# Layer attention: new places among the steps for a sequence's small operations, the first sequence's row maxima in six PSUM banks, and its chunk projected sooner

## The chip, the cores and the metric

The kernel runs on one core of one Trainium2 chip. The metric is the device time of one execution in microseconds (us), the median of several. Engines are named as in the profile: PE is TensorE's matmuls, PEld its weight loads, DVE VectorE, ACT ScalarE, POOL GpSimd, SP the engine that issues the DMAs.

## The reference, cut to what matters

Sixteen sequences of 256 tokens with 128 features go through four layers of (mamba, norm, attention, norm, feed-forward), then a mixture of experts, a sparse attention and the experts again. The change touches the attention of the four layers and the order of two operations in every layer norm:

```python
for l in range(4):
    m = _mamba(x, ...)                                   # before the attention
    x = _ln(x + m, g1[l], be1[l])
    qkv = jnp.einsum('bsd,od->bso', x, W_qkv) + b_qkv     # 16 heads of 8 features
    scores = jnp.einsum('bhqd,bhkd->bhqk', q, k) * SCALE
    wts = jax.nn.softmax(scores, axis=-1)
    o = jnp.einsum('bhqk,bhkd->bhqd', wts, v)
    x = _ln(x + o @ W_ao.T + b_ao, g2[l], be2[l])
    x = x + gelu(x @ W_f1.T + b_f1) @ W_f2.T + b_f2
```

## The kernel before, in words

**What a sequence needs.** For each sequence `b` the attention does the following. `project_qk` multiplies queries and keys into PSUM bank 7, `evac_qk` adds the biases on the way out, POOL's `parts` splits the values into high and low parts, SP's `spill` writes them to a scratch in HBM and `scatter` reads them back as 24-row groups into one of four buffers `hqk[r]`. `row` multiplies queries by keys with the queries on the partitions, so that DVE can take the maximum over the keys for each of 16 heads (`two_maxima` over two banks at once, 1024 columns; `maxima` over one, 512 columns; `copied_maxima` over one that ACT's `copy_row` has moved to SBUF). POOL's `split_max` splits the maxima, PE's `maxima` transposes them into bank 7, ACT's `max_rows` copies them, SP's `send_max` sends them by two DMAs into two further rows of `hqk[r]`. `score` then multiplies keys by queries and these rows, so that the maximum is subtracted, ACT's `exps` takes the exponentials (1024 columns at a time, eight per sequence), and PE's `values` multiplies them by the values (four groups of 16 matmuls into bank 6), which `project_v` and `lay_v` made by way of bank 7. ACT's `raw` copies the sums, PE's `sums` spreads the denominators in bank 7, ACT's `reciprocal` takes a logarithm and an exponential of its negative, POOL's `divide` multiplies, PE's `out` projects into bank 7, DVE's `add_out` adds to `xa`.

**Steps and places.** `heads` runs one step per sequence, 0 to 15: step 0 apart, twelve in a loop of three times four, 13 to 15 apart. A step has eight places, p = 0 to 7. At each, PE issues four `row` matmuls of two heads of a sequence one or two ahead (banks 0 and 1) and four `score` matmuls of two heads of the sequence itself (banks 2 and 3, or 4 and 5), and then one small operation. At even p one `two_maxima` frees banks 0 and 1; at odd p `maxima` frees bank 0 and `copy_row` bank 1. So `row` at p waits for the maxima of p-1. All engines run their instructions in the order of the program, and every hand-over is a semaphore wait, so an operation's place is its place in each engine's queue. Bank 7 has one user at a time: q and k, v, denominators, transposed maxima and output take turns.

**The places before.** PE: `project_v(b+1)` at 0, `values(b-1, 3)` at 1, `project_qk(b+3)` at 2, `values(b, 0)` at 3, `sums(b-1)` at 4, `values(b, 1)` and `maxima(b+1)` at 5, `values(b, 2)` at 6, `out(b-1)` at 7. DVE: `lay_v` at 0, `evac_qk` at 3 (two instructions of 256 columns), `add_out` at 7. ACT: `raw` at 1, both halves of `reciprocal` at 4, `max_rows` after the exponentials of 5. POOL: `copy_x`, `split_max`, `parts`, `divide`. SP: `spill(b+3)`, `send_max(b+1)`, `scatter(b+3)`.

**Ahead of the steps.** q and k of sequences 0 to 2 and v of 0 are projected in hooks inside the norm before the attention (PE hooks at quad and chunk (0,2), (1,0), (1,2), (1,3), ACT's at (0,3), (1,1), (1,3)). In the norm, DVE multiplies each chunk (line 1740, or its `dst` form) and then scales and shifts it (line 1745); it takes the multiplication of the next chunk ahead of that. Then come all 16 heads' rows of sequence 0 and the first 8 of sequence 1, in banks 0 and 1 only, and `maxima(0)` among sequence 1's.

## Time and profile before

| | |
|---|---|
| times of the kernel before | 2674.94, 2678.55, 2682.89 us (median 2678.55) |
| the profiled execution's own time | 2679.11 us |
| its span | 2677.4 us, mean granted TensorE clock 0.908 of full |
| PE, PEld busy | 80%, 52% of the span |
| DVE, ACT, POOL busy | 62%, 60%, 26% |
| DMA, mean over the span | 64 GB/s |

The span is the whole program, with stages that have different limits. The four layers' head attention begins (first `row`) at 150, 598, 1046 and 1493 us and takes about 265 us each time. A timeline row reads: start, duration, engine, line, operation, output<-inputs, shape, count, and in brackets how long the engine had been idle and what ended that.

### The profile page before, as it was taken

How to read it: one execution, taken by the hardware profiler on the slowest of the kernel's cores; microseconds unless marked ns; L12 is line 12 of the kernel's file. 1: busy time of each engine (PE TensorE's matmuls, PEld its weight loads, DVE VectorE, ACT ScalarE, POOL GpSimd, SP SyncE). 2: the span in 40 equal slices, each digit the busy share in tenths (PEclk: the TensorE clock that was granted, in tenths of full speed). 3: DMA queues.
4: the chain of work that ended last, by engine and by line, in shares of the span. 5: the costliest groups of instructions: out<-in, count | busy, mean ns of one | idle time of the engine just before them, and what ended most of it. 6: DMA issues, size and time to landing. Idle time of an engine off the chain costs nothing.

```text
span 2677.4 us, 49462 instructions
## 1 busy us (share of the span) xinstructions
PE 2136.1 (80%) x15147; PEld 1401.1 (52%) x15147; DVE 1664.4 (62%) x2491; ACT 1618.9 (60%) x2604; POOL 700.9 (26%) x980
## 2 busy tenths in 40 slices
PE   6968889987888896888899688887877478886795
PEld 4534445643444663444475344454666347775584
DVE  4557775656775765777475577756643267767541
ACT  6447778745777763777784477886544214454461
POOL 0113221022231102223101233211757130004664
PEclk8969999996999997899999699998988789997897
DMA  3033320013331002333000333204141201004223
GB/s 114 10 96 107 110 74 7 9 45 92 110 100 50 16 0 81 94 100 108 20 9 10 96 97 112 81 7 88 46 118 53 70 0 32 1 9 93 79 90 128
DMA packets 116930, 171.73 MB, mean 64 GB/s; under 512 B 13728, under 2 KB 75168, under 8 KB 116512
## 3 DMA queue, kind: packets, MB, share of 16 engines
q1 hardware_dynamic: 107552, 150.66, 19.9%
q0 software_dynamic: 9216, 19.02, 2.0%
q8 instruction: 88, 1.44, 0.2%
q14 instruction: 74, 0.61, 0.1%
HBM read 85.19 MB, written 82.35 MB: 63 GB/s over the span
## 4 chain that ended last, share of the span: by engine, by line
PE 49%; DVE 14%; POOL 11%; issue 10%; DMA 6%; ACT 6%; SPq 1%; DVEq 1%; ACTq 0%; POOLq 0%
PE ps L829 8%; DVE hmx L1883 6%; POOL back_scratch L2420 6%; PE ps L861 5%; POOL slot_scratch L2415 5%; DMA hqk<-hmt 3%; PE ps L877 2%; ACT hrow L1489 2%; PE ps L762 2%; PE ps L726 2%; PE ps L732 2%; PE ps L677 2%; PE ps L683 2%; PE ps L1257 1%; PE ps L1149 1%
## 5 line engine op out<-in xcount | busy, mean ns | idle before, releaser
L1468 ACT ACTIVATE hpt<-ps 128x1024 f32<-128x1024 f32 x512 | 518.5, 1020 | 57.3 <-PE ps L848 56.8
L829 PE MATMUL ps<-hqk 24*128 24x256 f32 x2048 | 287.1, 361 | 154.9 <-DVE hmx L1883 92.0
L829 PEld LDWEIGHTS ps<-hqk 24*128 24x128 f32 x2048 | 173.3, 208 | 368.3 <-DVE hmx L1883 207.6
L1883 DVE TENSOR_REDUCE hmx<-ps 128x4 f32<-128x1024 f32 x256 | 312.8, 1222 | 62.2 <-PE ps L829 60.0
L861 PE MATMUL ps<-hpt,hvx 128*32 128x256 f32 x4096 | 296.2, 410 | 21.8 <-ACT hpt L1468 21.2
L1876 DVE TENSOR_REDUCE hmx<-ps 128x2 f32<-128x512 f32 x256 | 177.3, 693 | 158.9 <-PE ps L829 158.9
L848 PE MATMUL ps<-hqk 26*128 26x256 f32 x2048 | 271.0, 346 | 2.8 <-ACT hpt L1468 1.6
L1489 ACT ACTIVATE hrow<-ps 128x512 f32<-128x512 f32 x256 | 151.9, 593 | 188.1 <-PE ps L829 188.1
L1892 DVE TENSOR_REDUCE hmx<-hrow 128x2 f32<-128x512 f32 x256 | 176.1, 688 | 40.1 <-ACT hrow L1489 29.9
L2420 POOL DMA_INDIRECT back_scratch<-ys,xslot x160 | 153.2, 958 | 86.8 <-issue 47.9
L848 PEld LDWEIGHTS ps<-hqk 26*128 26x128 f32 x2048 | 161.9, 196 | 22.3 <-ACT hpt L1468 16.5
L861 PEld LDWEIGHTS ps<-hpt,hvx 128*32 128x32 f32 x4096 | 111.8, 114 | 115.2 <-ACT hpt L1468 35.0
L2415 POOL DMA_INDIRECT slot_scratch<-xtok,slot_i x128 | 131.6, 1028 | 62.4 <-issue 38.4
L2360 POOL CAST hhl<-hmx 128x32 fp32r<-128x32 f32 x64 | 13.4, 209 | 404.6 <-DVE hmx L1892 404.6
L2312 POOL MEMSET hqk<- 128x1024 f32 x16 | 14.5, 952 | 390.1 <-PE ps L732 390.1
L1740 DVE TENSOR_TENSOR unit<-ps,rstd 128x512 f32<-128x512 f32 x64 | 44.2, 690 | 104.0 <-ACT rstd L1372 103.2
L2350 POOL TENSOR_TENSOR hon<-hraw,hrec 128x512 f32<-128x512 f32 x64 | 81.4, 1271 | 93.3 <-ACT hrec L1482 93.3
L877 PE MATMUL ps<-hraw,spread 128*128 128x512 f32 x128 | 74.1, 662 | 39.3 <-DVE hqk L1900 39.3
L677 PE MATMUL ps<-streams,center 128*128 128x512 f32 (+1 forms) x192 | 96.0, 623 | 9.4 <-SPq L549 5.1
L2331 POOL COPY hxs<-streams 128x256 f32 (+1 forms) x64 | 25.4, 396 | 298.0 <-PE ps L822 273.2
L1439 ACT ACTIVATE hidh<-ps,mw 128x512 fp32r<-128x512 f32 x128 | 89.4, 698 | 19.9 <-PE ps L789 19.9
L683 PE MATMUL ps<-sq,average 128*128 128x512 f32 x192 | 96.4, 601 | 3.6 <-ACT sq L1358 3.3
(326 smaller groups left out, 5342.9 us busy)
## 6 DMA issues: line engine op xcount, KB each, us to landing
hqk_scratch<-hqks SPq DMA_DIRECT2D x64, 768.0 KB, 3.2
hqk<-hqk_scratch SPq DMA_DIRECT2D x256, 192.0 KB
slot_scratch<-filler SPq DMA_DIRECT2D x10, 1040.0 KB, 15.7
xslot<-slot_scratch SPq DMA_DIRECT2D x20, 520.0 KB, 4.2
yback<-back_scratch SPq DMA_DIRECT2D x32, 256.0 KB, 4.4
mw<-mw_in SPq DMA_DIRECT2D x10, 516.5 KB, 3.5
w12raw<-w_in SPq DMA_DIRECT2D x1, 2560.0 KB, 9.3
back_scratch<-ys,xslot POOLq DMA_INDIRECT x160, 2.2
```

Of the source, the lines that this page charges most:

```text
L677: mm(ps[:, k, :], center[:], src[:, ds(c * CH, CH)], start=True, stop=True).then_inc(ln_cen, 1)
L683: mm(ps[:, 4 + k % 2, :], average[:], sq[:, k % 2, :], start=True, stop=True).then_inc(ln_var, 1)
L829: return mm(ps[:, o % 2, qt * SEQ:(qt + 1) * SEQ], hqk[r][32 * g:32 * g + 24, j, 0, qt * P:(qt + 1) * P], hqk[r][32 * g:32 * g + 24, j, 1, ...
L848: return mm(ps[:, 2 + g, kt * SEQ:(kt + 1) * SEQ], hqk[r][32 * g:32 * g + 26, j, 1, kt * P:(kt + 1) * P], hqk[r][32 * g:32 * g + 26, j, 0, ...
L861: last = mm(ps[32 * g:32 * g + 32, 6, (j // 2) * SEQ:(j // 2 + 1) * SEQ], hvx[r][:, kt, g, j, :], hpt[:, j, g, kt, :], start=j % 2 + kt == ...
L1468: A(hpt[:, j, g:g + 2, :, :], ps[:, 2 + g:4 + g, :], ACT.Exp, scale=QSCALE).then_inc(hd_exp, 1)
L1489: A(hrow[:, o // 4 % 2].rearrange("p t k -> p (t k)"), ps[:, 1, :], ACT.Copy).then_inc(hd_max[1], 1)
L1876: V.tensor_reduce(hmx[:, r, :, 4 * g + j], ps[:, o % 2, :].rearrange("p (t k) -> p t k", t=2), AX.X, ALU.max).then_inc(hd_max[0], 1)
L1883: V.tensor_reduce(hmx[:, r].rearrange("p t (g j) -> p g t j", j=4)[:, g:g + 2, :, j], ps[:, bank:bank + 2, :].rearrange("p x (t k) -> p x ...
L1892: V.tensor_reduce(hmx[:, r, :, 4 * g + j], hrow[:, o // 4 % 2], AX.X, ALU.max).then_inc(hd_red, 1)
L2415: G_.indirect_dma_start(slot_d, bass.IndirectOffsetOnAxis(slot_i[:, c, t:t + 1], 0), xtok[c][:, t, :], None).then_inc(sent, 16)
L2420: G_.indirect_dma_start(back_d, bass.IndirectOffsetOnAxis(xslot[:, g * 4 + b, D:D + 1].bitcast(I32), 0), ys[:, g % 4, b, :], None).then_in ...
```

## The change

It gives the small operations new places, splits `reciprocal` in two, merges `evac_qk`'s two instructions, lets sequence 0's rows use banks 0 to 5, moves one ACT hook, and turns the norm's order on DVE. The loop is now two times four steps (2 to 9), the others are written out. The diff without its context and without the new `second` parameter in the headers:

```diff
@@ heads @@
-            step(0, 0, first=True)
-            with eng.Fori(0, 3) as i:
+            step(0, 0, first=True, second=True)
+            step(1, 1, second=True)
+            with eng.Fori(0, 2) as i:
                 for k in range(4):
-                    step(i * 4 + (1 + k), (1 + k) % 4)
+                    step(i * 4 + (2 + k), (2 + k) % 4)
+            step(10, 2)
+            step(11, 3)
+            step(12, 0)
@@ tensor: step @@
-                        if p == 0 and n1:
-                            pe.wait_ge(hd_mt, nth(hd_mt, B))
-                            pe.wait_ge(hd_ao, nth(hd_ao, B - 2))
-                            project_v(b + 1)
+                        if p == 0 and n3:
+                            if first:
+                                pe.wait_ge(hd_mt, nth(hd_mt, B))
+                            else:
+                                pe.wait_ge(hd_v, nth(hd_v, B))
+                            project_qk(b + 3)
                         if p == 1 and not first:
                             values(b - 1, 3, (r + 3) % 4)
-                        if p == 2 and n3:
-                            pe.wait_ge(hd_v, nth(hd_v, B + 1))
-                            project_qk(b + 3)
+                        if p == 2 and not second:
+                            if n3:
+                                pe.wait_ge(hd_q, nth(hd_q, B + 3, 1))
+                            else:
+                                pe.wait_ge(hd_v, nth(hd_v, B))
+                            out(b - 2)
                         if p == 3:
                             values(b, 0, r)
                         if p == 4 and not first:
-                            if n3:
+                            if second:
                                 pe.wait_ge(hd_q, nth(hd_q, B + 3, 1))
-                            elif n1:
-                                pe.wait_ge(hd_v, nth(hd_v, B + 1))
                             else:
                                 pe.wait_ge(hd_ao, nth(hd_ao, B - 2))
                             sums(b - 1)
                         if p == 5:
-                            values(b, 1, r)
                             if n1:
                                 if first:
                                     pe.wait_ge(hd_q, nth(hd_q, B + 3, 1))
                                 else:
                                     pe.wait_ge(hd_ln, nth(hd_ln, B - 1))
                                 maxima(b + 1)
-                        if p == 6:
+                            values(b, 1, r)
+                        if p == 6 and n1:
+                            pe.wait_ge(hd_mt, nth(hd_mt, B + 1))
+                            project_v(b + 1)
+                        if p == 7:
                             values(b, 2, r)
-                        if p == 7 and not first:
-                            if n1:
-                                pe.wait_ge(hd_mt, nth(hd_mt, B + 1))
-                            else:
+                            if not n1:
                                 pe.wait_ge(hd_ln, nth(hd_ln, B - 1))
-                            out(b - 1)
+                                out(b - 1)
@@ tensor: sequence 0's rows @@
-                    rows(0, o, 0)
+                    if o % 2 == 0:
+                        pe.wait_ge(hd_max[0], nth(hd_max[0], l * BATCH, o // 2 - 3))
+                    row(o, 0, 0, 6)
+                    row(o, 0, 1, 6).then_inc(hd_am, 1)
+                pe.wait_ge(hd_bo, nth(hd_bo, l))
+                maxima(0)
                 pe.wait_ge(hd_scat, every(hd_scat, l * BATCH + 1))
                 for o in range(8):
-                    if o == 2:
-                        pe.wait_ge(hd_bo, nth(hd_bo, l))
-                        maxima(0)
                     rows(1, o, 1)
@@ scalar @@
-                def reciprocal(b):
+                def logarithm(b):
...
+                def reciprocal(b):
+                    B = l * BATCH + b
                     act.wait_ge(hd_ln, nth(hd_ln, B))
                     A(hrec[:], hrec[:], ACT.Exp, scale=-1.0).then_inc(hd_rec, 1)
...
+                        if p == 5 and n1:
+                            max_rows(b + 1)
                         exps(b, p)
                         if p == 1 and not first:
                             raw(b - 1)
                         if p == 4 and not first:
+                            logarithm(b - 1)
+                            if not n1:
+                                reciprocal(b - 1)
+                        if p == 7 and not first and n1:
                             reciprocal(b - 1)
-                        if p == 5 and n1:
-                            max_rows(b + 1)
...
                 evac_qk(2)
-                copy_row(0, 3)
-                copy_row(0, 7)
...
-                copy_row(0, 11)
-                copy_row(0, 15)
...
-                norm(l * 2 + 1, hooks={(0, 3): begin[0], (1, 1): begin[1], (1, 3): begin[2]})
+                norm(l * 2 + 1, hooks={(0, 2): begin[0], (1, 1): begin[1], (1, 3): begin[2]})
@@ vector @@
-                    ahead(0)
-                    for k in range(4):
-                        if k < 3:
-                            ahead(k + 1)
-                        affine(k)
+                    if dst is None:
+                        for k in range(4):
+                            ahead(k)
+                            affine(k)
+                    else:
...
-                    for a, bias in enumerate(("bq", "bk")):
-                        V.tensor_scalar(hqk32[:, a, :], ps[:, 7, a * SEQ:(a + 1) * SEQ], T(bias), None, ALU.add)\
-                         .then_inc(hd_q, 1)
+                    V.tensor_tensor(hqk32[:], ps[:, 7, :].rearrange("p (a n) -> p a n", a=2),
+                                    T("bq", 0, 2).unsqueeze(2).broadcast_to([P, 2, SEQ]), ALU.add).then_inc(hd_q, 2)
...
-                        if p == 0 and n1:
+                        if p == 0 and n3:
+                            evac_qk(b + 3)
+                        if p == 2 and not second:
+                            add_out(b - 2)
+                        if p == 6 and n1:
                             lay_v(b + 1, (r + 1) % 4)
-                        if p == 3 and n3:
-                            evac_qk(b + 3)
-                        if p == 7 and not first:
+                        if p == 7 and not n1:
                             add_out(b - 1)
...
-                for o in range(0, HEADS, 4):
-                    two_maxima(0, o, 0)
-                    maxima(0, o + 2, 0)
-                    copied_maxima(0, o + 3, 0)
+                for o in range(0, HEADS, 2):
+                    two_maxima(0, o, 0, o % 6)
+                dve.sem_inc(hd_max[1], 4)
+                dve.sem_inc(hd_red, 4)
@@ gpsimd: step @@
-                    if n2:
-                        copy_x(b + 2)
+                    if not second:
+                        divide(b - 2)
+                    if n3:
+                        parts(b + 3)
                     if n1:
                         split_max(b + 1, (r + 1) % 4)
-                    if n3:
-                        parts(b + 3)
-                    if not first:
+                    if n2:
+                        copy_x(b + 2)
+                    if not n1:
                         divide(b - 1)
```

## Rows read from the trace of the kernel before

**Rows 1.** The chain that ended last, shares of the span by engine.

```profile
PE 49%; DVE 14%; POOL 11%; issue 10%; DMA 6%; ACT 6%; SPq 1%; DVEq 1%; ACTq 0%; POOLq 0%
```

**Rows 2.** Windows, steps 2 to 13, four layers: length, engines' busy time, granted clock, DMA.

```profile
209.24:391.18 181.94, 148.72 (x1726) 77.72 (x1726) 139.94 (x190) 140.71 (x193) 53.54 (x92) 0.97 0.35 102
...
1550.65:1730.49 179.84, 145.86 (x1724) 76.73 (x1725) 140.10 (x190) 140.65 (x193) 53.53 (x92) 0.99 0.35 103
sum 728.19, PE 595.13 PEld 311.54 DVE 559.50 ACT 563.32 POOL 214.11; mean PE 148.78 PEld 77.88 DVE 139.88 ACT 140.83 POOL 53.53
```

**Rows 3.** Timeline of PE in step 5 of the first layer.

```profile
254.57 0.39 PE L829 MATMUL ps<-hqk 24*128 24x256 f32 x2 [0.53 <-DMA hqk<-hmt]
...
256.42 0.39 PE L829 MATMUL ps<-hqk 24*128 24x256 f32 x2 [0.69 <-DVE hmx L1883]
...
257.86 0.38 PE L829 MATMUL ps<-hqk 24*128 24x256 f32 x2
...
258.29 0.70 PE L816 MATMUL ps<-streams,tw 128*128 x2
...
262.58 1.12 PE L877 MATMUL ps<-hraw,spread 128*128 128x512 f32 x2 [0.93 <-DVE hqk L1900]
263.64 0.39 PE L829 MATMUL ps<-hqk 24*128 24x256 f32 x2
...
265.54 0.38 PE L829 MATMUL ps<-hqk 24*128 24x256 f32 x2
...
267.45 0.38 PE L829 MATMUL ps<-hqk 24*128 24x256 f32 x2
...
269.52 0.38 PE L829 MATMUL ps<-hqk 24*128 24x256 f32 x2 [0.49 <-DMA hqk<-hmt]
```

**Rows 4.** Timeline of DVE in the same step.

```profile
255.14 1.23 DVE L1883 TENSOR_REDUCE hmx<-ps 128x4 f32<-128x1024 f32 x1 [0.31 <-PE ps L829]
256.28 0.41 DVE L1906 COPY hvx<-ps 128x256 f32<-128x256 f32 x1
256.95 0.69 DVE L1876 TENSOR_REDUCE hmx<-ps 128x2 f32<-128x512 f32 x1 [0.26 <-PE ps L829]
...
261.58 0.86 DVE L1900 TENSOR_SCALAR hqk<-ps,tw 128x256 f32<-128x256 f32 x2
```

**Rows 5.** Timeline of ACT in the same step.

```profile
263.74 0.60 ACT L1480 ACTIVATE hrec<-ps 128x512 f32<-128x512 f32 x1 [0.88 <-PE ps L877]
...
264.90 0.58 ACT L1489 ACTIVATE hrow<-ps 128x512 f32<-128x512 f32 x1
...
266.28 0.36 ACT L1461 ACTIVATE hmt<-ps 32x256 fp32r<-32x256 f32 x1
```

**Rows 6.** The costliest groups: DVE's multiplication of PSUM by SBUF.

```profile
L1740 DVE TENSOR_TENSOR unit<-ps,rstd 128x512 f32<-128x512 f32 x64 | 44.2, 690 | 104.0 <-ACT rstd L1372 103.2
```

**Rows 7.** Timeline of PE ahead of step 0 and in it, first layer.

```profile
150.20 0.80 PE L829 MATMUL ps<-hqk 24*128 24x256 f32 x4 [1.96 <-DMA hqk<-hqk_scratch]
...
165.43 0.80 PE L829 MATMUL ps<-hqk 24*128 24x256 f32 x4 [0.86 <-ACT hrow L1489]
...
173.03 0.58 PE L829 MATMUL ps<-hqk 24*128 24x256 f32 x2 [0.86 <-ACT hrow L1489]
```

**Rows 8.** Timeline of SP's queue ahead of step 0.

```profile
155.57 1.54 SPq L588 DMA_DIRECT2D hqk<-hqk_scratch  x4
162.27 0.34 SPq L579 DMA_DIRECT2D hqk_scratch<-hqks  x1
165.57 1.55 SPq L588 DMA_DIRECT2D hqk<-hqk_scratch  x4
```

**Rows 9.** Windows: steps 0 and 1 at the lower clock; step 14.

```profile
173.03:200.50 27.47, 24.05 (x186) 13.17 (x190) 16.84 (x22) 15.09 (x19) 3.83 (x8) 0.50 0.20 60
391.18:404.52 13.34, 10.88 (x126) 5.68 (x126) 6.46 (x10) 11.30 (x15) 1.72 (x3) 1.00 0.01 4
```

**Rows 10.** Timeline of PE where the feed-forward of the first layer begins.

```profile
437.86 0.79 PE L787 MATMUL ps<-fxh,wf1h 128*128 128x512 f32 x1 [3.09 <-DVE fxl L1774]
```

More of the change, by code:

```diff
@@ L596, in send_max, with step @@
                                      hmt[16 * part:16 * part + 16].bitcast(F32)).then_inc(hd_mx, 16)
-                def step(b, r, first=False, n1=True, n2=True, n3=True):
+                def step(b, r, first=False, second=False, n1=True, n2=True, n3=True):
                     if n3:
@@ L824, in project_v, with row @@
                     last.then_inc(hd_vp, 1)
-                def row(o, r, qt):
+                def row(o, r, qt, banks=2):
                     j, g = ORDER[o] // 4, ORDER[o] % 4
-                    return mm(ps[:, o % 2, qt * SEQ:(qt + 1) * SEQ],
+                    return mm(ps[:, o % banks, qt * SEQ:(qt + 1) * SEQ],
                               hqk[r][32 * g:32 * g + 24, j, 0, qt * P:(qt + 1) * P],
@@ L890, in value_bias, with step @@
                     last.then_inc(hd_bp, 1)
-                def step(b, r, first=False, n1=True, n2=True, n3=True):
+                def step(b, r, first=False, second=False, n1=True, n2=True, n3=True):
                     B = l * BATCH + b
@@ L1489, in copy_row, with step @@
                     A(hrow[:, o // 4 % 2].rearrange("p t k -> p (t k)"), ps[:, 1, :], ACT.Copy).then_inc(hd_max[1], 1)
-                def step(b, r, first=False, n1=True, n2=True, n3=True):
+                def step(b, r, first=False, second=False, n1=True, n2=True, n3=True):
                     for p in range(8):
@@ L1509, in head_attention, with last_reciprocal @@
                     return [lambda: evac_qk(0), first_v, lambda: evac_qk(1)]
+                def last_reciprocal():
+                    logarithm(15)
+                    reciprocal(15)
                 if part == "end":
-                    return [lambda: reciprocal(15)]
+                    return [last_reciprocal]
                 evac_qk(2)
-                copy_row(0, 3)
-                copy_row(0, 7)
                 act.wait_ge(hd_bp, nth(hd_bp, l))
                 A(hbo[:], ps[:, 7, 0:1], ACT.Identity, bias=T("bo")).then_inc(hd_bo, 1)
-                copy_row(0, 11)
-                copy_row(0, 15)
                 max_rows(0)
@@ L1753, in ahead @@
                         multiply(k)
-                    ahead(0)
-                    for k in range(4):
-                        if k < 3:
-                            ahead(k + 1)
-                        affine(k)
+                    if dst is None:
[3 more added lines that the diff above has]
+                    else:
+                        ahead(0)
+                        for k in range(4):
+                            if k < 3:
+                                ahead(k + 1)
+                            affine(k)
                 if hooks:
@@ L1914, in add_out, with step @@
                                            xa[:, ds(b * SEQ, SEQ)], ALU.add, ALU.add).then_inc(hd_ao, 1)
-                def step(b, r, first=False, n1=True, n2=True, n3=True):
+                def step(b, r, first=False, second=False, n1=True, n2=True, n3=True):
                     for p in range(8):
@@ L2363, in split_max, with step @@
                       .then_inc(hd_mlo, 1)
-                def step(b, r, first=False, n1=True, n2=True, n3=True):
+                def step(b, r, first=False, second=False, n1=True, n2=True, n3=True):
+                    if not second:
+                        divide(b - 2)
+                    if n3:
+                        parts(b + 3)
+                    if n1:
+                        split_max(b + 1, (r + 1) % 4)
                     if n2:
                         copy_x(b + 2)
-                    if n1:
-                        split_max(b + 1, (r + 1) % 4)
-                    if n3:
-                        parts(b + 3)
-                    if not first:
+                    if not n1:
                         divide(b - 1)
```

## Prediction

> **What bounds the kernel now.** I read the shares of the chain first: PE holds 49% of it, DVE 14% and ACT 6% [rows 1]. Then I cut the attention into stretches. Steps 2 to 13 of the four layers take 728.2 us together, 27% of the span, with PE busy for 595.1, ACT for 563.3 and DVE for 559.5 of them [rows 2]. No engine is full, so the order of hand-overs sets the step.
>
> The timeline shows it. Step 5 runs from 254.57 to 269.52, 14.95 us, and 48 such steps are 717.6 us; the other 10.6 us go with stretches at the lower of TensorE's two levels, 1.2 in place of 2.4 GHz (the granted clock is 0.97 in the first layer and 0.99 in the last) [rows 2, 3]. Rows and scores of one place take PE 0.43 us (257.86 to 258.29). The rest is a cycle through banks 0 and 1: PE starts at 254.57, `two_maxima` starts at 255.14 and takes 1.23 us, PE starts the next place at 256.42. So an even place costs 1.85 us and has 1.4 us for a small operation. An odd place costs 1.44 us: its short reduction and ACT's copy free the banks by about 1.3 us, and `values` takes 1.0 us behind the 0.43 [rows 3, 4]. Four of each would make 13.16 us. The step loses the other 1.8 us where a small operation stands in the wrong place:
> - at 4, `sums` waits 0.93 us for `evac_qk`, which stands behind the reductions of 3. The place costs 0.43 + 0.93 + 1.06 and a little, 2.5 us;
> - at 5, ACT's copy for bank 1 stands behind logarithm and exponential (264.90). 1.90 us;
> - at 6, `values` in an even place, waiting for ACT. 1.91 us;
> - at 7, `out`, and then a wait of 0.49 us for the DMA of the maxima. 2.07 us [rows 3, 5].
>
> **The steady step after.** I lay the new order out from PE's start of place 0, with durations from the rows.
> - 0: `project_qk` ends at 0.43 + 1.07 = 1.5 (its matmuls begin at 258.29 in the trace; the 1.07 is that of `sums`, 262.58 to 263.64 [rows 3]). `two_maxima` runs 0.57 to 1.80, `evac_qk` from 1.7. Its new form, one addition of 512 columns from PSUM with SBUF, isn't in the trace. Below stands 0.69 us, the multiplication of the same shape [rows 6]; above, the 0.86 us of the two instructions that it replaces [rows 4]. I take 0.69, the row of its own shape: it ends at 2.4, and the reduction of place 1 comes up at 1.85 + 0.53 = 2.4. With 0.86 each step costs 0.17 us more, 8 us in all. Place 0: 1.85.
> - 1: `values`, 1.44. `raw` follows `exps` on ACT and delays the exponentials of 2 by nothing that PE waits for.
> - 2: `out(b-2)` fits in 1.4 us; it needs POOL's `divide(b-2)`. The exponential for it now ends some 1.1 us into the step, `divide` takes 1.3 us, so it is there at 2.4 and PE asks at 3.7. `add_out` runs behind `two_maxima`, where DVE has 0.6 us free. 1.85.
> - 3: `values`, 1.44.
> - 4: `sums` waits for nothing (`add_out` ended at 5.5, PE asks at 7.0). ACT's logarithm starts 1.16 us behind `sums` as now and takes 0.60 [rows 3, 5]: 8.2 to 8.8. The copy of place 5 comes up at 9.0. 1.85.
> - 5: the transposes now stand ahead of `values` and wait for the logarithm: PE asks at 8.9. They add about 0.45 us. ACT's `max_rows` (0.36 us [rows 5]) slips in before the exponentials of 5. 0.43 + 0.1 + 0.4 + 1.0 = 1.95.
> - 6: `project_v` fits, `lay_v` behind `two_maxima`. 1.85.
> - 7: `values`, 1.44. The maxima were copied at 9.8 us, 3.7 us before the next step; the DMAs took 2.9 us from there in step 5 (266.64 to 269.52). Their wait goes.
>
> The sum is 13.67 us. Behind it ACT (11.7 us busy in a step) and DVE (11.7) keep some 2 us. POOL's `parts` is done at 5.2, the spill lands by 8.5, `scatter` follows `send_max` at 11.1 and took 6.7 us ahead of step 0 (155.57 to 162.27 [rows 8]), so it lands at 4.1 of the next step, before the next spill asks at 5.2 and PE at 6.6. Three hand-overs have only 0.1 us of room (`evac_qk`, the logarithm, the exponential beside the next step's first scores), so I take 13.75. The cases above that are priced below.
>
> 48 steps: 48 x (14.95 - 13.75) = **57.6 us**. Of the 10.6 us at the lower clock I take back half, **5.3**: PE's busy share of a step rises from 12.2 in 14.95 to 12.2 in 13.75. The bounds are 0 and 10.6.
>
> A page rule on this: the Trainium skill (TensorE: Matmul & The Clock Gate, "HAM oscillation") says that gaps in PE's work bring the clock down and sustained work brings it back. By it the lower stretches would all go, and the term would be 10.6.
>
> **Ahead of step 0.** From 150.20 to 165.43 PE makes sequence 0's rows: 3.8 us for four heads [rows 7]. With six banks DVE takes eight `two_maxima` at 1.14 us from start to start (255.14 to 256.28 [rows 4]), 9.2 us in all, and PE and ACT don't hold it. It also starts sooner, since `affine(0)` comes before `multiply(1)` and ACT's hook one chunk earlier: 1.5 us for PE's projection, and 3.4 for the first spill. But the next step of the path is sequence 1's rows, which need its scatter. That ended at 162.2 [rows 8], and hangs on `evac_qk(1)`, which moves by 1.5 us only. So they start at 160.7, not 165.43; eight heads take 7.6 us as now [rows 7], which makes step 0 possible at 168.3. It also needs `send_max(0)`, and on SP that stands behind `scatter(2)`, now at 164.1 and 1.55 us long [rows 8]: issued at 165.7 and landed 2.9 us later it is 168.6. If its packets queue behind the scatter's, it is some 6.5 us behind 164.1, 170.6. Before, step 0 began at 173.03. I take 170.0, a gain of 3.0; the bounds are 2.4 and 4.7. Four layers: **12 us**.
>
> The Trainium skill (DMA: Bandwidth & Descriptors, "Queues, rings and completion order") says that the DMAs of one queue share a ring on each DMA engine and start in order there. By it step 0 starts at 170.6 and the four layers give 9.6 us.
>
> **Steps 0 and 1** run at 1.2 GHz: 27.5 us from 173.03 with PE busy for 24.1 and the clock at 0.50 [rows 9]. There PE bounds, and its work doesn't shrink. Step 0 gets 0.5 us longer (`values` leaves place 6 and lengthens 7), step 1, which ends at the full clock, 1.2 us shorter: 0.7 x 4 = **3 us**, with bounds of -4 and +12 for when the clock rises.
>
> **The rest.** Step 14 has rows in its first half only and took 13.34 us [rows 9]; its end waits for the maxima's DMA, whose copy comes 0.75 us sooner: **3 us**. Step 15 is ACT's exponentials in a row: nothing. In the norm, DVE's new order gives the last chunk's `affine` 0.5 us sooner and starts the feed-forward's split sooner; PE waited 3.09 us for it [rows 10], but the second half still needs the eighth multiplication. 0.7 us per layer, **3 us**, between 0 and 6. POOL's and SP's new orders cost nothing: both idle for two thirds of a step.
>
> **Sum.** 57.6 + 5.3 + 12 + 3 + 3 + 3 = 84 us off the profiled execution's 2679.1: **2595 us**. That execution is 0.6 us above the median of 2678.55, so the forecast stands for the median too.
>
> **Rivals.**
> - **ACT comes late to place 4.** If the exponentials of 3 and 4 run 0.5 us late, the logarithm, the transposes, `values` and place 6 all shift, as no other work stands in front of them on PE. A step is then 14.3: 48 x 0.65 + 18 = 49 us, about 2630. For: the new wait on the logarithm has `values` queued behind it. Against: ACT has 0.6 us idle before the copies of 1 and 3. Chance 0.18.
> - **The new wait eats all.** `out(b-2)` at 2 waits for `divide`, which stands behind an exponential that ACT now does last. 1.2 us of room; if it comes 2.5 us late the step is 14.95 again and only the first stretch's gain stays: about 2665, and with a little more it is no change. Chance 0.09, half of it within 0.3%.
> - **The clock's rule.** With PE denser the clock stays up (10.6 us, not 5.3) and rises 3 us sooner in each layer's first steps, a gain of 1.5 us each: 2679 - 84 - 5 - 6 = 2584. Chance 0.12.
> - **Slower: the clock stays down.** Six banks let PE end sequence 0's rows sooner and stand idle longer until the scatter lands. The clock fell just there before [rows 7, 9]. A step of the new order at 1.2 GHz costs PE about 21.4 us (8 x 0.75, four `values` of 1.87, q and k, `out` and `sums` of 2.0 each, v and transposes 1.6), 7.7 more than 13.7. The gain of 84 us is gone after 11 such steps, about three more in each layer. With four more in each it is 2595 + 16 x 7.7 = 2718. For: the rise came only 27 us into the steps. Against: it came with PE busy in 88% of that time, and the new order leaves no larger gap. Chance 0.06.
> - The forecast itself: 0.55.
>
> **Range.** 0.17 us more in `evac_qk`, 0.65 us more in the step, or the small terms at their lower bounds reach 2630; a 13.55 us step with the whole 10.6 and the upper bounds 2568. So 2568 to 2630. A measurement of this kernel tells 0.3%, 8 us, from no change (the three times lie within 8 us). Faster 0.89, within 0.05, slower 0.06: 0.55, 0.18, 0.12 and half of 0.09; the other half; the last rival.
>
> **What would show it.** Right: a steady step of 13.6 to 13.9 us; no idle time of PE ahead of `sums` and ahead of place 0; `evac_qk` at 0.7 us; first rows of sequence 1 near 160.7 and step 0 near 170 in the first layer; a granted clock of 0.97 or more in steps 2 to 13. Wrong: PE waiting for ACT's logarithm ahead of the transposes, for `divide` ahead of `out`, or steps 2 and 3 at 0.50.

## The result and the profile after

The changed kernel takes 2567.90 us (median of four, 2560.49 to 2572.22) against 2680.72 us (2674.94 to 2686.37) of the kernel before on the same chip: a ratio of 0.9576, 95% interval 0.9545 to 0.9608. It is 113 us faster. The forecast was 84, and the range ended 0.1 us above the measured time. The profiled execution took 2567.65 us, its span is 2566.0 us, and its granted clock is 0.917 (0.908 before).

The chain that ended last, shares of the span by engine, of the changed kernel (compare [rows 1]):

```profile
PE 54%; DVE 18%; POOL 11%; issue 8%; DMA 4%; ACT 2%; SPq 1%; DVEq 1%; POOLq 0%; ACTq 0%
```

ACT falls from 6% to 2% and DMA from 6% to 4%. PE and DVE take a larger share of a shorter span.

The windows of steps 2 to 13 in the four layers of the changed kernel, with the columns of [rows 2]:

```profile
202.72:364.89 162.17, 142.50 (x1729) 75.81 (x1725) 140.42 (x180) 139.64 (x193) 54.04 (x92) 1.00 0.38 114
617.97:780.13 162.16, 142.50 (x1732) 75.82 (x1728) 140.43 (x180) 139.64 (x193) 54.07 (x92) 1.00 0.38 114
1037.14:1199.29 162.15, 142.49 (x1729) 75.81 (x1726) 140.42 (x180) 139.63 (x193) 54.06 (x92) 1.00 0.38 114
1453.93:1617.30 163.37, 144.01 (x1728) 76.53 (x1724) 140.44 (x180) 139.85 (x193) 54.04 (x92) 0.99 0.38 113
sum 649.85, PE 571.50 PEld 303.97 DVE 561.71 ACT 558.77 POOL 216.21; mean PE 142.87 PEld 75.99 DVE 140.43 ACT 139.69 POOL 54.05
```

They took 728.19 us before and take 649.85 now. Work is the same on DVE and ACT to within 1%; what went is idle time, and on PE 24 us of busy time. Of these, 5 are the step's own (in step 5, at the full clock, PE was busy for 12.07 us before and is for 11.97 now); most of the others are time of matmuls that had run at the lower of the clock's two levels. Three layers run these steps at full clock throughout, 13.51 us per step.

What PE waited for in these steps of the first layer (us in total, times, longest), first after, then before:

```profile
PE ps L833 <- DVE hmx L1904: 19.7, 48, 1.3
```

```profile
PE ps L829 <- DVE hmx L1883: 12.9, 25, 1.3
PE ps L877 <- DVE hqk L1900: 8.7, 10, 0.9
PE ps L829 <- DMA hqk<-hmt: 6.2, 11, 1.1
PE ps L861 <- ACT hpt L1468: 4.4, 11, 0.4
```

This is the plainest view of the change. Before, PE waited above all for four kinds of thing. Now one is left: 48 waits, four in each of twelve steps, for the maximum of 1024 columns that frees banks 0 and 1.

PE in step 5 of the changed kernel, 243.27 to 256.78 (compare [rows 3]; here L833 are rows, L865 `values`, L881 `sums`, L874 the transposes of the maxima):

```profile
243.27 0.38 PE L833 MATMUL ps<-hqk 24*128 24x256 f32 x2
...
243.71 0.70 PE L820 MATMUL ps<-streams,tw 128*128 x2
...
245.12 0.38 PE L833 MATMUL ps<-hqk 24*128 24x256 f32 x2 [0.28 <-DVE hmx L1904]
...
250.28 1.13 PE L881 MATMUL ps<-hraw,spread 128*128 128x512 f32 x2
251.69 0.39 PE L833 MATMUL ps<-hqk 24*128 24x256 f32 x2 [0.28 <-DVE hmx L1904]
...
252.18 0.39 PE L874 MATMUL ps<-ident,hhl 128*32 128x128 f32 x2
252.49 1.07 PE L865 MATMUL ps<-hpt,hvx 128*32 128x256 f32 x16
253.50 0.38 PE L833 MATMUL ps<-hqk 24*128 24x256 f32 x2
...
256.78 0.39 PE L833 MATMUL ps<-hqk 24*128 24x256 f32 x2
```

`sums` (250.28) and the next step's first rows (256.78) wait for nothing. The starts of L833 give the places: 1.85, 1.44, 1.85, 1.44, 1.84, 1.81, 1.85, 1.43. Nearly all of the gain of 1.44 us lies at places 4 and 7, which took 2.50 and 2.07 before, where the waits of `sums` and for the DMA of the maxima are gone. No run moves one small operation alone, so this share-out is read from the rows. DVE and ACT in the same step (compare [rows 4, 5]):

```profile
245.03 0.69 DVE L1920 TENSOR_TENSOR hqk<-ps,tw 128x512 f32<-128x512 f32 x1
245.65 0.69 DVE L1897 TENSOR_REDUCE hmx<-ps 128x2 f32<-128x512 f32 x1
```

```profile
251.46 0.59 ACT L1489 ACTIVATE hrec<-ps 128x512 f32<-128x512 f32 x1
```

The merged `evac_qk` takes 0.69 us. The logarithm starts 1.18 us behind `sums` and ends at 252.05; the transposes come at 252.18.

Ahead of step 0 in the first layer, PE and then SP's queue in the changed kernel (compare [rows 7, 8]):

```profile
147.13 1.18 PE L833 MATMUL ps<-hqk 24*128 24x256 f32 x12 [0.50 <-DMA hqk<-hqk_scratch]
...
158.51 0.80 PE L833 MATMUL ps<-hqk 24*128 24x256 f32 x4
...
168.55 0.58 PE L833 MATMUL ps<-hqk 24*128 24x256 f32 x2 [3.29 <-DMA hqk<-hmt]
```

```profile
161.61 1.55 SPq L592 DMA_DIRECT2D hqk<-hqk_scratch  x4
163.20 1.31 SPq L599 DMA_DIRECT2D hqk<-hmt  x2
```

Step 0 begins at 168.55 instead of 173.03, and what it waits for has changed: ACT's copy before, the DMA of the maxima now. The second sequence's transfers move by more than PE's head start. SP's queue in the changed kernel:

```profile
148.68 0.35 SPq L583 DMA_DIRECT2D hqk_scratch<-hqks  x1
152.05 1.54 SPq L592 DMA_DIRECT2D hqk<-hqk_scratch  x4
```

Before, the spill went out at 150.34 and its scatter at 155.57 [rows 8]:

```profile
150.34 0.35 SPq L579 DMA_DIRECT2D hqk_scratch<-hqks  x1
```

So the spill is 1.66 us sooner and the scatter 3.52, since 3.37 us lie between the two instead of 5.23.

The whole of it, cut at the same marks in both traces (us, all four layers; a mark is the start of a row of PE's timeline, the last score's that of its last pair of matmuls):

| stretch | before | after | difference | forecast |
|---|---|---|---|---|
| first rows of layer 1 | 150.20 | 147.13 | -3.07 | |
| a feed-forward's last matmul to the next layer's first rows (three) | 338.78 | 328.60 | -10.18 | |
| first rows to step 0 (four) | 91.29 | 85.66 | -5.63 | -12 for these three |
| steps 0 and 1 | 143.49 | 128.77 | -14.72 | -3 |
| steps 2 to 13 | 728.19 | 649.85 | -78.34 | -62.9 |
| step 14 to the last score | 88.70 | 88.32 | -0.38 | -3 |
| last score to the feed-forward's last matmul | 282.43 | 284.70 | +2.27 | -3 |
| behind the layers | 854.3 | 853.0 | -1.35 | 0 |

### The profile page after: what moved, and what is told of

Same layout as the page of the kernel before. It is cut to its first block, busy times and chain, and to the rows that moved or that the text cites. A ratio compares the mean times of both kernels' runs of the same rounds, so it can differ in the third digit from the quotient of the medians.

```text
span 2566.0 us, 49078 instructions
## 1 busy us (share of the span) xinstructions
PE 2093.0 (82%) x15147; PEld 1387.5 (54%) x15147; DVE 1664.4 (65%) x2423; ACT 1601.8 (62%) x2588; POOL 704.4 (27%) x980
## 3 DMA queue, kind: packets, MB, share of 16 engines
q0 software_dynamic: 9216, 19.02, 2.1%
## 4 chain that ended last, share of the span: by engine, by line
PE 54%; DVE 18%; POOL 11%; issue 8%; DMA 4%; ACT 2%; SPq 1%; DVEq 1%; POOLq 0%; ACTq 0%
DVE hmx L1904 11%; PE ps L865 10%; PE ps L833 9%; POOL back_scratch L2444 6%; POOL slot_scratch L2439 5%; PE ps L766 2%; PE ps L730 2%; PE ps L736 2%; PE ps L681 2%; PE ps L687 2%; PE ps L1266 1%; PE ps L1158 1%; PE ps L1243 1%; PE ps L717 1%; PE ps L718 1%
## 5 line engine op out<-in xcount | busy, mean ns | idle before, releaser
L833 PE MATMUL ps<-hqk 24*128 24x256 f32 x2048 | 275.2, 354 | 145.5 <-DVE hmx L1904 123.1
L1904 DVE TENSOR_REDUCE hmx<-ps 128x4 f32<-128x1024 f32 x272 | 330.8, 1225 | 72.9 <-PE ps L833 66.0
L833 PEld LDWEIGHTS ps<-hqk 24*128 24x128 f32 x2048 | 166.3, 202 | 357.5 <-DVE hmx L1904 232.1
L865 PE MATMUL ps<-hpt,hvx 128*32 128x256 f32 x4096 | 284.7, 397 | 0.0
L1501 ACT ACTIVATE hrow<-ps 128x512 f32<-128x512 f32 x240 | 143.3, 597 | 144.7 <-PE ps L833 144.7
L1897 DVE TENSOR_REDUCE hmx<-ps 128x2 f32<-128x512 f32 x240 | 166.3, 693 | 76.5 <-PE ps L833 76.5
L1913 DVE TENSOR_REDUCE hmx<-hrow 128x2 f32<-128x512 f32 x240 | 165.0, 688 | 12.0
L865 PEld LDWEIGHTS ps<-hpt,hvx 128*32 128x32 f32 x4096 | 109.1, 111 | 89.1 <-issue 22.3
L2439 POOL DMA_INDIRECT slot_scratch<-xtok,slot_i x128 | 131.1, 1024 | 62.4 <-issue 38.4
L1756 DVE TENSOR_TENSOR unit<-ps,rstd 128x512 f32<-128x512 f32 x64 | 44.1, 689 | 84.5 <-ACT rstd L1381 84.5
L1869 DVE TENSOR_TENSOR hidl<-hid,hidh 128x1024 fp32r<-128x1024 f32 x64 | 78.4, 1224 | 29.1 <-ACT hid L1449 29.0
L2353 POOL COPY hxs<-streams 128x256 f32<-128x256 f32 (+1 forms) x64 | 25.4, 397 | 242.5 <-PE ps L826 224.2
L1376 ACT ACTIVATE logv<-ps,acol 128x512 f32<-128x512 f32 x96 | 65.8, 685 | 41.4 <-PE ps L687 40.9
```

Source lines behind the costliest of these rows:

```text
L833: return mm(ps[:, o % banks, qt * SEQ:(qt + 1) * SEQ], hqk[r][32 * g:32 * g + 24, j, 0, qt * P:(qt + 1) * P], hqk[r][32 * g:32 * g + 24, j ...
L865: last = mm(ps[32 * g:32 * g + 32, 6, (j // 2) * SEQ:(j // 2 + 1) * SEQ], hvx[r][:, kt, g, j, :], hpt[:, j, g, kt, :], start=j % 2 + kt == ...
L1501: A(hrow[:, o // 4 % 2].rearrange("p t k -> p (t k)"), ps[:, 1, :], ACT.Copy).then_inc(hd_max[1], 1)
L1897: V.tensor_reduce(hmx[:, r, :, 4 * g + j], ps[:, o % 2, :].rearrange("p (t k) -> p t k", t=2), AX.X, ALU.max).then_inc(hd_max[0], 1)
L1904: V.tensor_reduce(hmx[:, r].rearrange("p t (g j) -> p g t j", j=4)[:, g:g + 2, :, j], ps[:, bank:bank + 2, :].rearrange("p x (t k) -> p x ...
L1913: V.tensor_reduce(hmx[:, r, :, 4 * g + j], hrow[:, o // 4 % 2], AX.X, ALU.max).then_inc(hd_red, 1)
```

## Experiments

Each kernel is the changed one with the edit shown. Its ratio is to the kernel before on its own chip (four kernels shared one and its runs of before: 2681.86, 2865.0 and 2858.47 us); the changed kernel's is 0.9576, where before took 2680.72 us, and 0.9605 [0.9581, 0.9628] on the last chip. On the second and third of these chips the part behind the layers is longer (spans of 2733 us and up), while the layers end within 3 us of the same mark (the changed kernel's last feed-forward matmul at 1713.03 and 1710.07 us), so marks of the layers are compared across all. "End of layers" is that mark; before it is 1823.08. A mark comes from one profiled execution, which need not lie at the kernel's median: on the last chip that of the changed kernel took 2736.02 us, 10.6 below its median, and that with the old hook 2766.17, 7.8 above its own. The same kernel's steps 0 and 1 took 128.7 us in one of its two profiled executions and 133.1 in the other. A difference of some us between two runs' marks is therefore not shown to come from the edit.

**Undoing one part at a time.** First the places alone: two banks, the norm's old order with the old ACT hook, and two `evac_qk` instructions, that is, the edits of the next three experiments together.

> Only the new places in the steps (and the split logarithm); two banks for sequence 0's rows, the norm's order, ACT's hook and the two instructions of evac_qk are as before. Theory A (the places carry it: they make the step 13.5 us and, by filling PE's gaps, also bring the clock up sooner): steps 2 to 13 take 13.5 to 13.7 us each at a granted clock of 1.00, steps 0 and 1 together about 32 to 34 us, time 2590 (about 30 us of the 113 are the other parts). Theory B (the clock's gain comes from six banks and the earlier start): steps 13.6 us, but steps 0 and 1 again 35.5 us or more and the clock rising 27 us into them, time 2605 or more.

2601.99 us, ratio 0.9701 [0.9683, 0.9719]; end of layers 1748.52; the steady step is 13.53 us. The places bring 80 of the 113 us, and all of the steady step.

The second undoes the six banks, with DVE's and ACT's part of them:

```diff
...
-                    row(o, 0, 0, 6)
-                    row(o, 0, 1, 6).then_inc(hd_am, 1)
-                pe.wait_ge(hd_bo, nth(hd_bo, l))
-                maxima(0)
+                    rows(0, o, 0)
...
```

> The changed kernel with sequence 0's rows in two banks again, all else new. Before the result: six banks move sequence 1's rows by 1.5 us at most, since these hang on the second scatter; with two banks 16 heads take 15.2 us from 147.1, so sequence 1's rows begin at 162.3 in place of 158.5 and step 0 at 170 in place of 168.5: 1.4 us per layer, 6 us in all, time 2574. The rival (six banks change when the clock rises): a difference of more than 12 us, and another interval between step 0 and the rise of the clock than 15 us (layers 2 to 4) and 23 us (layer 1).

0.9618 [0.9602, 0.9634], 2580.35 us, some 12 us slower than the changed kernel; end of layers 1730.16. The first rows to step 0 take 90.7 us against 85.7 in the four layers, as [rows 7] would have it: these 5 us are the banks'. Of the other 12 of the 17 us at the end of the layers, 7 are in steps 0 and 1 and 4 in step 2 of layer 1, whose first three steps took 19.02, 17.29 and 17.20 us from place 0 to place 0, with the clock low again until 215.8 us. That part was not forecast, and since steps 0 and 1 of one kernel differ by 4.4 us between two executions, the run doesn't show how much of it is the banks'.

The third undoes the norm's order and the hook:

```diff
-                    if dst is None:
-                        for k in range(4):
-                            ahead(k)
-                            affine(k)
...
-                norm(l * 2 + 1, hooks={(0, 2): begin[0]
+                norm(l * 2 + 1, hooks={(0, 3): begin[0]
```

> The changed kernel with DVE's order in the norms and ACT's hook as before. By the prediction's working the first scatter lands 3.4 us later and all behind it 1.5 us later per layer, and the feed-forward starts 0.7 us later: about 9 us in all, time 2577. If the 2 us per layer by which the feed-forward became shorter also hang on this order, it is 15 us or more.

0.9663 [0.9647, 0.9679], 2590.48 us, 22.6 us slower; end of layers 1737.03. This is the largest miss among the parts.

The fourth puts the two 256-column additions back:

```diff
-                    V.tensor_tensor(hqk32[:], ps[:, 7, :] ...
+                    for a, bias in enumerate(("bq", "bk")):
+                        V.tensor_scalar(hqk32[:, a, :], ...
```

> The changed kernel with evac_qk as two instructions of 256 columns again. They take 0.86 us in place of 0.69. If DVE had no room at place 0, place 1 begins its reduction 0.17 us late and the step is 13.69 us: 48 x 0.17 = 8 us, time 2576. If PE's values hide it (place 1 ends with PE's 1.0 us of values, not with the reduction), the step grows by less than 0.1 us and the time by under 4 us.

0.9591 [0.9572, 0.9609], 2570.88 us: not told apart from the changed kernel. Ten steady steps in the four layers take 541.2 us against 540.5, 0.02 us per step. The merged form was worth nearly nothing: `evac_qk` takes 0.87 us again (from 242.75), and PE's places 0 and 1 are still 1.86 and 1.45 us long (rows at 241.03, 242.89 and 244.34).

**The order and the hook apart,** on the last chip, beside the changed kernel itself.

> The changed kernel itself, on the chip of the next three, so that they can be compared with it. Expected: a ratio to the kernel before of 0.957 to 0.961, first score of layer 1 at 168.5 us, end of the last layer's feed-forward at 1713 us, steady step 13.52 us. If the ratio lies at 0.961 or above, this chip's last part (the experts) is longer, and the marks of the layers decide.

0.9605 [0.9581, 0.9628], 2746.58 us; first score at 167.41, end of layers 1710.07, 13.51 us per step.

> The changed kernel with only the old order in the norm (the next chunk's multiplication ahead of a chunk's affine), ACT's hook in its new place. Order and hook together cost 24 us by the end of the last layer. Theory A (the order is the larger part, since it acts in both norms and decides when the first projection's input is there): 14 to 20 us later than the changed kernel, with the first rows 1.5 to 2.5 us later and the feed-forward's start 0.7 us later behind the last score. Rival H (the hook is what brings the first projection forward): 4 to 8 us, all of it behind the last score, first rows as in the changed kernel at 147.1 us. Rival C (neither alone: the clock): both this and the next cost under 6.

> The changed kernel with only ACT's hook back behind chunk (0,3), the norm's order new. Theory A: 4 to 8 us, the first rows 0.5 to 1 us later and nothing behind the last score. Rival H: 14 to 18 us, first rows 2 us or more later. Rival C: under 6 here too, so the 24 us of both together were the clock's.

The old order: 0.9702 [0.9680, 0.9724], 2774.17 us, end of layers 1736.92. The old hook: 0.9641 [0.9620, 0.9661], 2758.34 us, end of layers 1731.68. By the medians the order costs 28 us and the hook 12; the intervals of the two ratios don't overlap, so the order is the larger part, as theory A has it. At the end of the layers it is 27 and 22, but there the profiled executions stand 10.6 us below the one median and 7.8 above the other. Both sizes were forecast too small, and theory A's small delay of the first rows without the new hook (0.5 to 1 us) did not come: it is 3.1 us in layer 1, which was rival H's sign. The parts each do something of their own. Whether they add isn't settled: both together cost 23 us on another chip. The old order's 26.9 us lie at: first rows of layer 1 1.6, feed-forward to first rows 12.5, first rows to step 0 1.9, steps 5.9, behind the last score 5.0.

The order's mechanism, in layer 2. First DVE and PE of the changed kernel on the last chip, then of the old order (L1756 multiplies, L1761 scales and shifts, L820 is the first projection):

```profile
545.74 0.69 DVE L1756 TENSOR_TENSOR unit<-ps,rstd 128x512 f32<-128x512 f32 x1 [4.47 <-ACT rstd L1381]
546.47 0.55 DVE L1761 TENSOR_SCALAR streams<-unit,mw 128x512 f32<-128x512 f32 x1
...
547.07 0.70 PE L820 MATMUL ps<-streams,tw 128*128 128x256 f32 x2 [0.61 <-DVE streams L1761]
...
562.73 0.83 PE L833 MATMUL ps<-hqk 24*128 24x256 f32 x4
```

```profile
551.46 0.69 DVE L1756 TENSOR_TENSOR unit<-ps,rstd 128x512 f32<-128x512 f32 x1 [4.47 <-ACT rstd L1381]
553.18 0.69 DVE L1756 TENSOR_TENSOR unit<-ps,rstd 128x512 f32<-128x512 f32 x1 [1.02 <-ACT rstd L1381]
553.79 0.54 DVE L1761 TENSOR_SCALAR streams<-unit,mw 128x512 f32<-128x512 f32 x1
554.38 0.70 PE L820 MATMUL ps<-streams,tw 128*128 128x256 f32 x2 [2.19 <-DVE streams L1761]
...
571.34 0.89 PE L833 MATMUL ps<-hqk 24*128 24x256 f32 x12 [0.26 <-DVE streams L1761]
```

From the first multiplication to PE's projection it is 1.33 us against 2.92, and to the first rows 16.99 against 19.88. PE's wait, 2.19 us in place of 0.61, is the whole first difference. Behind it this run shows a low stretch of the clock (555.0 to 558.4, granted 0.50) that the changed kernel doesn't have; the kernel before had the same wait of 2.19 us and no low stretch there, so that stretch is no part of what the change gained.

The hook's mechanism is another. PE's first projection of layer 2 and its first rows, in the kernel before and in the changed one with the old hook:

```profile
580.77 0.70 PE L816 MATMUL ps<-streams,tw 128*128 128x256 f32 x2 [2.19 <-DVE streams L1745]
...
598.16 0.80 PE L829 MATMUL ps<-hqk 24*128 24x256 f32 x4 [2.05 <-DMA hqk<-hqk_scratch]
```

```profile
553.13 0.70 PE L820 MATMUL ps<-streams,tw 128*128 128x256 f32 x2 [0.60 <-DVE streams L1761]
...
570.33 1.22 PE L833 MATMUL ps<-hqk 24*128 24x256 f32 x12 [1.02 <-DMA hqk<-hqk_scratch]
```

With the old hook the first scatter comes late, and PE waits for it; with the new one (the first block above, 562.73) it doesn't. From the projection to the first rows it is 17.39 and 17.20 us there and 15.66 here. With the old hook it is also 4.5 to 5.4 us from the second spill to its scatter on SP, and 3.3 in each layer with the new one (4.8 to 5.7 in the kernel before). Why that time falls, the runs don't show: with the new places alone, which keep the old hook, it is 5.4 in the first layer and 3.3 in the others.

**What the step is made of.** Both halves of the reciprocal at place 4 in every step:

```diff
-                            if not n1:
-                                reciprocal(b - 1)
-                        if p == 7 and not first and n1:
-                            reciprocal(b - 1)
+                            reciprocal(b - 1)
```

> The changed kernel with logarithm and exponential both at place 4 again. ACT then runs 0.53 us of exponential between the logarithm and the copy that frees bank 1; max_rows and the exponentials of 5 come 0.3 us or more later. Expected: place 5 grows by 0.2 to 0.5 us in each step, 48 x 0.35 = 17 us, time 2585. If the copy's room (0.3 us idle ahead of it) hides most: under 10 us. The clock: if the granted clock falls below 1.00 in steps 2 to 13 with gaps of this size, the lower stretches of the kernel before hang on PE's gaps in the step.

0.9601 [0.9585, 0.9618], 2751.35 us, and the steady step stays at 13.51 to 13.52. So splitting the two halves is not what shortened the step: ACT is busy for 11.6 of its 13.5 us, and the exponential fills idle time that ACT had ahead of the copy of place 5 (0.30 us in the changed kernel's step 5) and after the exponentials behind it (0.79). The cost that I had expected was not there.

**The queue ahead of step 0.** The maxima of sequence 0 are sent ahead of sequence 2's scatter:

```diff
                     spill(b)
+                    if b == 2:
+                        send_max(0, 0)
                     scatter(b, b)
-                send_max(0, 0)
```

> The changed kernel with send_max(0) issued ahead of scatter(2) on SP. In the changed kernel PE waits 3.0 to 3.3 us for the DMA of the maxima ahead of step 0. If the wait is the place in SP's queue, step 0 begins at 165.3 to 165.6 in the first layer in place of 168.55, 12 us in all, time 2556. Rival: step 0 runs at the lower clock anyway and the shorter idle stretch changes when it rises; then the gain differs from 12 us by more than 4.

> The changed kernel with the maxima of sequence 0 sent ahead of the scatter of sequence 2. Theory (SP's queue order is what step 0 waits for): 2.2 us sooner per layer, 9 to 11 us by the end of the last layer, and a ratio 0.003 to 0.004 below that of the changed kernel beside it. Rival (the clock takes it back: PE starts the steps sooner but has to run as many at the lower level): under 4 us, no difference that 5 rounds can tell.

0.9575 [0.9553, 0.9597] (2742.97 us) and 0.9590 [0.9575, 0.9605] (2742.46 us). SP's queue and PE in the first of them:

```profile
159.05 1.62 SPq L599 DMA_DIRECT2D hqk<-hmt  x2
161.85 1.55 SPq L592 DMA_DIRECT2D hqk<-hqk_scratch  x4
```

```profile
166.34 0.58 PE L834 MATMUL ps<-hqk 24*128 24x256 f32 x2 [0.85 <-ACT hrow L1502]
```

Step 0 comes 2.2 us sooner per layer (first rows to first score 76.8 and 77.2 us in the four layers, 85.7 and 85.8 without), and no DMA holds it. That part is shown in both runs. In total little of it is left to see: beside each other the medians are 4.1 us apart (2742.46 against 2746.58), and the intervals overlap. The marks say no more: end of layers 1701.97 in one run and 1711.76 in the other, against 1710.07. The rival of the second expectation has the size about right (under 4 us) but not the place: steps 0 and 1 took 132.8 us in the repeat, where the changed kernel beside it took 133.1. The 8.6 us gained were lost in its trace elsewhere, 3.9 in step 14 of layer 4 (the clock low from 1615.9 to 1626.2), 3.7 behind the last scores and 3 ahead of the first rows.

**The clock at the first steps.** Matmuls without use fill PE's idle time ahead of step 0 (bank 6, nothing reads it):

```diff
+                def fill(n):
+                    mm(ps[:, 6, 0:n], center[:], res[:, 0:n], start=True, stop=True)
...
+                    if o % 2 == 1 and o > 6:
+                        fill(128)
+                fill(CH)
+                fill(CH)
...
+                    if o % 4 == 1:
+                        fill(SEQ + P)
+                    if o % 4 == 3:
+                        fill(SEQ)
+                fill(CH)
```

> The changed kernel with idle matmuls added on PE between the rows of sequences 0 and 1 and ahead of step 0 (128 to 512 columns each, a constant matrix times the input, into bank 6, which the first values overwrite). They do no work of the kernel; they only stand where PE waited. Theory (the clock falls because PE idles ahead of step 0, and steps 0 and 1 are slow because of it): the clock is up at step 0 or within 5 us of it, steps 0 and 1 take 27 to 29 us in place of 34.2 (layer 1) and 31.5 (others), and the time falls by 12 to 22 us, to about 2550. Rival (the clock's fall and rise don't hang on what PE does there): the clock rises as late as before, and the added matmuls, which don't all fit into the gaps at the lower clock, cost 0 to 2 us per layer: 2568 to 2576.

0.9612 [0.9596, 0.9627], 2754.11 us: no gain. In layer 1 the clock rose at 158.1 us, but fell again at 168.3, at the end of PE's wait of 2.55 us for the maxima's DMA, and steps 0 and 1 took as long (34.34 us). In the other layers it was up when step 0 began, fell 4.6 to 4.8 us later, and the four layers' steps 0 and 1 took 133.5 us. With the maxima sent first as well:

> Both: idle matmuls ahead of step 0 and send_max(0) ahead of scatter(2). If the gains are independent, 24 to 34 us off the changed kernel's 2568: about 2538. If the idle matmuls at the lower clock are now longer than the wait that they fill (2.6 us of them ahead of step 0 where the wait is gone), about 8 us of that is lost again: 2546.

0.9559 [0.9544, 0.9575], 2736.89 us. Steps 0 and 1 of layers 1 and 2, first in the changed kernel, then in this one, then layer 2 of the kernel before:

```profile
168.55:202.72 34.17, 28.07 (x264) 14.78 (x264) 22.25 (x28) 20.94 (x28) 6.88 (x14) 0.66 0.25 80
586.46:617.97 31.51, 24.62 (x266) 13.01 (x266) 22.20 (x28) 20.94 (x28) 6.89 (x14) 0.76 0.28 87
```

```profile
167.79:200.44 32.65, 26.43 (x266) 13.56 (x265) 22.18 (x29) 21.05 (x28) 6.87 (x14) 0.74 0.30 92
587.78:616.73 28.95, 22.11 (x267) 11.78 (x266) 22.19 (x29) 20.80 (x28) 6.86 (x14) 0.88 0.30 97
```

```profile
620.98:656.50 35.52, 30.06 (x266) 15.62 (x267) 23.54 (x32) 22.29 (x29) 8.10 (x15) 0.67 0.21 69
```

The four layers' steps 0 and 1 take 119.9 us here, and 128.7 to 139.0 in every other kernel with the new places. So what the clock is worth there can be had, at least in part, by leaving PE no long idle time ahead. It has a price: first rows to step 0 take 82.4 us, some 5 more than with the maxima sent first alone. This is the fastest version by ratio, though its profiled execution is the slowest of its four (2744.19 us). Its interval lies below the changed kernel's on the last chip, but the two did not run beside each other, and it doesn't separate from the maxima sent first alone.

## Why the prediction was wrong, and where it was right

The direction, the two largest terms as the largest and the mechanism of the steady step held. Four terms were too small, and the sum went 0.1 us past the range's stated lower end. That end is itself an error of adding: a 13.55 us step (67.2), the whole 10.6, 18.8 ahead of step 0, 12 in steps 0 and 1, 3 in step 14 and 6 in the norm make 117.6 us and 2561.5, not 2568, and the measured time lies inside that. Two smaller sums are off as well, without effect: place 5's terms make 1.93, not 1.95, and the step at the lower clock 21.1, not 21.4.

1. **The steady step: right in mechanism, 11.5 us too small.** The layout gave 13.67 us; the trace has 13.51. The places came out to 0.01 us but for place 5: 1.81 instead of 1.95. The two transposes take 0.31 us (252.18 to 252.49) and start 0.06 late, where I had put 0.1 + 0.4. The further 0.08 us that I added for three hand-overs with 0.1 us of room was needed by none of them, and the experiments with two additions and with both halves at 4 show that the room is larger than I thought. 48 x (14.95 - 13.51) = 69.1, not 57.6.
2. **The clock inside steps 2 to 13: 9.2 us, not 5.3.** 78.34 - 69.1 is left for it. Before, the granted clock was 0.96 to 0.99; after it is 1.00 in three layers and 0.99 in the fourth, and in the changed kernel's second trace no low stretch is left in any. I had taken half because I had no reason for another share. The rule of the Trainium skill (TensorE: Matmul & The Clock Gate, "HAM oscillation"), by which sustained work brings the clock back, gave 10.6; the first trace comes within 1.4 us of it, the second agrees.
3. **Steps 0 and 1: the failed step.** I wrote "PE bounds, and its work doesn't shrink", and 3 us, with a bound of 12 "for when the clock rises". It was 14.7 in this execution, past the bound, and 10.4 in the changed kernel's second trace, so three to five times the forecast. PE's busy time in them fell (30.06 to 24.62 us in layer 2) because the clock rose some 15 us behind the start of step 0 in layers 2 to 4, and 23 in layer 1, instead of some 27 (in two layers with a short rise between). The new places work on both sides of that moment: the places alone brought them from 143.5 to 136.6 us, and the kernels that undo less than that lie between 131.9 and 139.0. How much of it is the denser work and how much the moment at which the steps start, the runs don't settle; the filled kernel with the maxima sent first shows that PE's idle time ahead acts on it.
4. **Ahead of step 0: 18.9 us, not 12,** 4.7 per layer, the upper bound of the forecast. Sequence 1's rows began at 158.51 instead of 160.7. I moved `evac_qk(1)` by 1.5 us and stopped there. Its spill did move by 1.66, but the scatter followed 3.37 us behind it where it had been 5.23, and those 1.9 us I had not seen. Ahead of the first rows of layers 2 to 4 it is 3.4 us per layer on average: 1.6 from PE's shorter wait in the norm and 1.8 because PE no longer waits for the first scatter. The step's new wait came as forecast: 3.29 us for the maxima's DMA, behind the scatter on SP. From the scatter's issue to step 0 it took 6.9 us (161.61 to 168.55), near the 6.5 of the case in which they queue. Sending them first took the wait away. Both fit the rule of the Trainium skill (DMA: Bandwidth & Descriptors, "Queues, rings and completion order") that one queue's DMAs start in order; no run tells that from two transfers sharing the same DMA engines.
5. **Step 14 and the feed-forward: nothing, not 6 us.** Step 14 went from 13.34 to 12.65 us in layer 1, but in layer 4 the clock was low in it (1618.6 to 1628.9 us) and that cost 4.0: from place 0 of step 14 to the last score it took 25.1 us there and 21.1 in layer 3. In the changed kernel's second trace that stretch is not low, and step 14 gains 0.5 to 0.7 us in each layer, near the forecast of 3 in all. The norm's order starts the feed-forward 0.7 us sooner than the old order does with the new places (24.61 us behind the last score against 25.33); the kernel before had 24.45, so the places cost there what the order gives.
6. **The rivals.** ACT was not late at place 4, `out` did not wait for `divide`, the clock did not stay down. The clock's rule, chance 0.12, was the one that happened, and it was too small too (11 us; the clock's part was about 9 in the steady steps and much of the 10 to 15 in the first two). That the total came so near the stated end is chance: step 14 and the feed-forward, forecast at 6 us, gave nothing in this execution.

## What to carry to other kernels

Lay out one steady period from the rows, each engine's queue by itself, and trust the layout: here seven of eight places were right to 0.01 us, and the step's error was the 0.14 us of the eighth and the 0.08 added for safety on top. A change that takes idle time from TensorE is to be priced at both levels of the clock in every stretch that ran at the lower one. An input that is ready sooner at the head of a chain is to be followed through each transfer that hangs on it: here 1.6 us less of waiting on TensorE came with 1.8 us more from the first DMA and 1.9 from the second. The bounds of a range are to be added up term by term, as the forecast is.

## What was not expected of the hardware

- One kernel's low stretches of the clock move between executions while the sum hardly does. The changed kernel's steps 0 and 1 took 128.7 us in one and 133.1 in the other, step 14 of layer 4 16.6 and 12.6, and its layers ended at 1713.03 and 1710.07. Two kernels' traces that differ by 4 us in one stretch need not differ by the edit.
- From the second spill's issue to its scatter's it is 4.8 to 5.7 us in the kernel before and 3.3 to 3.4 in the changed one, for the same bytes; what sets it stays open.
- Idle time of TensorE filled with matmuls of no use brought nothing by itself (0.9612) and shortened steps 0 and 1 to 119.9 us once the wait behind it was gone too.
